# A decoder of two layers on one core: the second attention's masked keys made in three steps (batch 0, batch 1, batches 2 and 3) instead of two

## What is computed

```python
x = x + _L0_attn_ref(_layernorm(x), ...)                        # chunked delta rule with decays
x = x + _L0_xattn_ref(_layernorm(x), ctx_1024, ctx_1024, ...)   # 16 heads, tanh layers for q, k, v
x = x + _L0_ffn_ref(_layernorm(x), ...)                         # 4 experts, best 2
x = x + _L1_attn_ref(_layernorm(x), ...)                        # latent attention, causal
x = x + _L1_xattn_ref(_layernorm(x), ctx_1024, ctx_1024, ...)   # 16 heads, causal
x = x + _L1_ffn_ref(_layernorm(x), ...)                         # 8 experts, best 2
```

```python
latent = x @ Wc_down
q = (latent @ Wq_up).reshape(Bsz, Tlen, N_HEAD, HEAD_DIM)
kv = latent @ Wkv_up
k, v = (kv[..., :HEAD_DIM], kv[..., HEAD_DIM:])
att = jnp.einsum('bthd,bsd->bhts', q, k) * scale
att = jnp.where(causal[None, None], att, -jnp.inf)
att = jax.nn.softmax(att, axis=-1)
y = jnp.einsum('bhts,bsd->bthd', att, v).reshape(Bsz, Tlen, C)
return y @ Wc_proj
```

## Time and profile before

| | us |
|---|---|
| median of 3 runs | 5426.35 |
| lowest and highest of them | 5419.66, 5430.18 |
| the profiled execution, its own time | 5424.35 |
| its span, first to last instruction | 5421.6 |

### The profile page before, as it was taken

The page is one execution under the profiler, slowest core; times in us unless marked ns, Lnnn a source line. Parts: engine busy times, 40 slices in busy tenths (PEclk is TensorE's granted clock), DMA queues, the critical chain, the costliest instruction groups (busy, mean ns, idle before and its releaser), DMA issues.

```text
span 5421.6 us, 105836 instructions
## 1 busy us (share of the span) xinstructions
PE 4688.4 (86%) x28201; PEld 3073.6 (57%) x28362; DVE 4177.1 (77%) x10963; ACT 2323.3 (43%) x4480; POOL 4005.8 (74%) x11220
## 2 busy tenths in 40 slices
PE   1059998999999899999989999898999999899998
PEld 1045664656566565656656565565656556565655
DVE  7068787787887778788787878778787887778788
ACT  0034444444444444444444444444444444444344
POOL 7878676786867678686767868677786867768686
PEclk7589999999999999999999999999999999999999
DMA  3000000000000000000000000000000000000000
GB/s 97 0 13 1 29 1 13 17 9 21 1 25 5 9 21 9 21 1 25 5 9 21 7 23 1 25 5 9 21 1 29 1 25 5 9 21 1 21 1 17
DMA packets 61879, 78.07 MB, mean 14 GB/s; under 512 B 11168, under 2 KB 53808, under 8 KB 61232
## 3 DMA queue, kind: packets, MB, share of 16 engines
q1 hardware_dynamic: 52784, 62.42, 3.5%
q10 hardware_dynamic: 8448, 8.39, 0.4%
HBM read 45.04 MB, written 8.46 MB: 10 GB/s over the span
## 4 chain that ended last, share of the span: by engine, by line
POOL 36%; PE 28%; DVE 17%; issue 11%; ACT 4%; POOLq 3%; DMA 0%; DVEq 0%; ACTq 0%; SPq 0%
POOL acc_c L584 12%; POOL arena L584 7%; POOL acc_a L584 3%; POOL acc_b L584 3%; PE bank L1280 3%; POOL acc_s L584 3%; POOL sl_t L584 3%; POOLq L583 3%; PE bank L1016 2%; DVE arena L2018 2%; PE bank L1187 2%; PE bank L1023 2%; PE bank L1140 2%; PE bank L1106 2%; ACT arena L779 2%
## 5 line engine op out<-in xcount | busy, mean ns | idle before, releaser
L1784 DVE TENSOR_REDUCE smax<-bank 128x4 f32<-128x512 f32 x768 | 524.4, 683 | 92.1 <-PE bank L1098 31.8
L766 ACT ACTIVATE arena<-bank 128x512 f32<-128x512 f32 x768 | 454.8, 592 | 248.4 <-PE bank L1106 242.6
L1788 DVE TENSOR_TENSOR arena<-bank,smax 128x512 f32<-128x512 f32 x768 | 530.8, 691 | 26.4
L1106 PE MATMUL bank<-ident,arena 128*128 128x128 f32 x3072 | 484.8, 280 | 45.1 <-ACT arena L753 28.1
L1092 PE MATMUL bank<-arena 64*128 64x512 f32 x1536 | 439.2, 648 | 64.4 <-ACT arena L790 28.0
L1187 PE MATMUL bank<-w,arena 128*128 128x512 f32 x1024 | 480.0, 599 | 14.0 <-DVE arena L1736 14.0
L1106 PEld LDWEIGHTS bank<-ident,arena 128*128 128x128 f32 x3072 | 345.7, 141 | 245.0 <-ACT arena L755 82.3
L1220 PE MATMUL bank<-w,arena 128*128 128x256 f32 x2048 | 454.1, 380 | 13.9 <-ACT arena L825 13.9
L753 ACT ACTIVATE arena<-arena,rstd 128x512 f32<-128x512 f32 x512 | 368.2, 719 | 201.4 <-DVE arena L1788 196.8
L1220 PEld LDWEIGHTS bank<-w,arena 128*128 128x128 f32 x2048 | 387.8, 190 | 90.3 <-issue 23.0
L584 POOL TENSOR_TENSOR acc_a<-acc_s,arena 128x32 f32<-128x32 f32 x1008 | 264.6, 262 | 171.6 <-DVE row L1347 47.2
(11 more groups left out here) (428 smaller groups left out, 11813.6 us busy)
## 6 DMA issues: line engine op xcount, KB each, us to landing
arena<-in_x_dram SPq DMA_DIRECT2D x35, 512.0 KB, 3.6
xn_next<-arena SPq DMA_DIRECT2D x17, 512.0 KB, 2.9
arena<-cum_dram SPq DMA_DIRECT2D x17, 512.0 KB, 3.6
arena<-in_ctx_dram SPq DMA_DIRECT2D x16, 512.0 KB, 3.7
out_dram<-arena ACTq DMA_DIRECT2D x16, 512.0 KB, 3.1
xn<-xn_next SPq DMA_DIRECT2D x15, 512.0 KB, 3.1
w<-in_L_ffn_w_dram SPq DMA_DIRECT2D x8, 512.0 KB
w<-in_L_ffn_w_dram SPq DMA_DIRECT2D x1, 1024.0 KB
```

Of the source, the lines that this page charges most:

```text
L766: act.activation(PT[:, v % 2], bank[3 + v % 2][:, :].rearrange("p (h q) -> p h q", h=QH), ACT.Copy).then_inc(S["pt"], 1)
L1106: ins = tr(bank[3 + v % 2][:, j * P:(j + 1) * P], Ssb[:, v % 4, j, :], ident[:, :])
L1784: dve.tensor_reduce(smax[:, u, :], sc, AX, ALU.max).then_inc(S["s_max"], 1)
L1788: dve.tensor_tensor(Ssb[:, u % 4], sc, smax[:, u, :].unsqueeze(2).broadcast_to([P, QH, P]), ALU.subtract).then_inc(S["s_sub"], 1)
```

## The change

ACT makes the masked keys of the second attention for batch 0 alone, then for batch 1 alone, then for batches 2 and 3 together: twelve activations instead of eight, three raises of `km` instead of two. PE waits for the raise that belongs to its batch. The third attention's masks count from the fifth raise on.

```diff
@@ -54,7 +54,7 @@
-    h_psum=6, h_act=6, lat_psum=1, lat=1, q_psum=6, q=6, k_psum=5, k_rows=1, km=6, v_psum=5, v=6,
+    h_psum=6, h_act=6, lat_psum=1, lat=1, q_psum=6, q=6, k_psum=5, k_rows=1, km=7, v_psum=5, v=6,
@@ -784,10 +784,9 @@
                     act.wait_ge(S["k_psum"], at(it, "k_psum", 3))
-                    for m in range(2):
-                        two = slice(2 * m, 2 * m + 2)
+                    for some in (slice(0, 1), slice(1, 2), slice(2, 4)):
                         for j in range(QH):
-                            ins = act.activation(KM[:, two, 0, j, :], heads(bank[3][:, :])[:, two, :], ACT.Identity, scale=halfmask[:, j:j + 1])
+                            ins = act.activation(KM[:, some, 0, j, :], heads(bank[3][:, :])[:, some, :], ACT.Identity, scale=halfmask[:, j:j + 1])
                         ins.then_inc(S["km"], 1)
@@ -1084,7 +1083,7 @@
-                            pe.wait_ge(S["km"], at(it, "km", KM_BEFORE[a_no] + (c if chunks > 1 else g // 2) + 1))
+                            pe.wait_ge(S["km"], at(it, "km", KM_BEFORE[a_no] + (c if chunks > 1 else min(g, 2)) + 1))
@@ -2040,7 +2039,7 @@
-KM_BEFORE = (0, 2, 4)
+KM_BEFORE = (0, 2, 5)
```

## The result

The changed kernel took **5454.65 us** (median of 6 runs, 5451.20 to 5457.48) where the kernel before took 5428.31 (6 runs, 5419.66 to 5431.64): a ratio of **1.0048**, 95% interval 1.0037 to 1.0059. That is slower than the forecast 5429 and beyond the range's 5439. The same kernel measured once more in a later series gave 5444.44 us (10 runs, 5440.63 to 5448.50) beside 5433.46 (13 runs): 1.0021, interval 1.0012 to 1.0031. So the change costs between 0.2 and 0.5%, and how much differs from series to series by more than either interval.

The account below looks back on a forecast made before the run. POOL's chain to `au` was taken as the bound, absorbing the 0.40 us gain in DVE's wait. Sum: 5424.35 profiled - 0.4 (pass without wait) + 3.1 (one more long pass) + 2.0 (median above profile) = 5429 us; range 5417 to 5439.

Parts of the forecast that it names:

- The bound of the kernel: From the first mixture's gates to `au`, POOL's chain sets the pace, about 145 us; time gained before DVE's wait is absorbed.
- rival 1: The wait for `au` does not absorb the gain: 0.40 us shorter per pass, 6.4 us in all, 5420; chance 0.08.
- The masks: Second attention on ACT: narrow masks take 387 ns, all twelve end at 3.66 us, later batches do not wait.
- The shift: Second attention's first scores start 0.40 us earlier in each pass, with ends of 0 and 0.72.
- the register row ahead of the first scores: Added register operation on PE, covered by the wait for ACT; register rows taken as 0, bounds 0 and 2.6 us.
- The idle time before L1147: PE's idle time before the third batch's normalized attention grows by 0.40 us, 1.29 to 1.69, just under 1.77.
- the alternating case: Part of rival 2: passes of 1.69 us idle tip, the next does not; 8 long passes for 5, 5435.
- The count of long passes: Five of 15 passes were long, about 320 us; the change was taken to add one more.
- The clock term: PE's lost clock behind the wait before line 1148: 3.1 us per long pass, one more taken, +3.1 us.
- Rival 2: PE's longer idle time before line 1148 tips the clock in more passes: 5435 or 5445; chance 0.22.
- rival 3: The shift clears two or three long passes, one of which came with DVE late: 5417 to 5420; chance 0.12.
- What I said would show it: DVE's wait for `au` up 0.40 us a pass to about 24 in all; no growth means DVE not earlier.

Follow-up runs that it names:

- the wide mask first: Changed kernel with its three mask steps reordered: batches 0 and 1 together, then 2, then 3; 5429.85 us, ratio 0.9994 to the kernel before.
- POOL late: Kernel before, with two unread additions on POOL right before it writes `au`; 5454.43 us, ratio 1.0046.
- the repeat: The changed kernel measured once more in a later series, nothing edited; 5444.44 us, ratio 1.0021.
- the change's waits filled: Changed kernel with six unread matmuls in PE's wait before the third batch's transposes in the third attention; 5434.09 us, ratio 1.0000.
- both places: Changed kernel with twelve unread matmuls in PE's wait before line 1148 and 18 instead of 14 in the first mixture; 5406.03 us, ratio 0.9964.
- one then three: Kernel before with masks still in two steps, batch 0 alone, then batches 1, 2 and 3 together; 5456.87 us, ratio 1.0037.
- the mixture's fill alone: Changed kernel with 18 instead of 14 unread matmuls in the first mixture, none before line 1148; 5457.49 us, ratio 1.0048.
- the third fill: Changed kernel with both places filled, plus four unread matmuls before the last mixture's gates; 5406.52 us, ratio 0.9964.

## Why the prediction was wrong

- **The bound of the kernel**: right. POOL's stretch to `au` is 145.61 us on the mean after the change (145.52 before) and stays in 145.3 to 146.0. A gain in front of it was not worth anything: rival 1 (5420) came in no run of these masks without a new fill.
- **The masks**: right. 383 ns for the forecast 387, 3.63 us for twelve where 3.66 was figured (the wide ones read 537 ns instead of 488 behind narrow ones, but start 0.36 us apart as before), no wait for the later batches, and ACT's added time free (the wide mask first: 0.9994).
- **The shift**: too small. 0.52 us for 0.40, inside its ends of 0 and 0.72. The masks gave 0.42 where 0.40 was figured; the handover to PE gave another 0.09, and no term stood for it. I had put the register row ahead of the first scores at 0, and it goes with a gain.
- **The idle time before L1147**: wrong through the shift. I figured 1.69 and called it just under the 1.77 that had lost the clock. It was 1.78 to 2.17 in the long passes of both profiles but one (3.38). With the right shift the sum would have read 1.29 + 0.52 = 1.81, above 1.77, and the alternating case the least to expect. Even 1.69 would hardly have held: 1.51 lost the clock in both passes that had it (POOL late).
- **The count of long passes**: this is the step that failed. I took one more (+3.1 us); of all 16 there were nine more in the first profile (four by PE's idle time, five late) and six more in the second (five and one), the last pass among them. The clock term of the sum was 3.1 us, and the added long passes took 30.6 of the first profile's 31.6 us and about 18 of the repeat's 19.9. The price of one, 3.1 us, was right: 2.8 by the events behind `au`, 2.9 by the pair of the repeat.
- **What the count rested on**: I argued that a long pass shifts what follows it, from the one pair 1.96 and 0.97. In the repeat a long pass follows a long one with 1.97 to 1.98 four times (its second, eighth, ninth and twelfth).
- **Rival 2** was the mechanism, and I gave it 0.22. Its two prices, 5435 and 5445, frame the repeat: 5426.35 x 1.0021 = 5438. The first measurement, 5426.35 x 1.0048 = 5452, lies beyond both, and its profile has five late passes more, for which no term of the sum stood, though the profile before had one and rival 3 named it.
- **Rival 3**: it did not show. The register rows cost nothing (the wide mask first, 0.9994).
- **What I said would show it**: the wait for `au` was to grow to about 24 us. It went to 17.7 and 19.9, which by my own words would have said that DVE did not arrive earlier. It did: late passes with no wait at all took it out of the sum. The wait of single passes was the sign to name, 1.0 us in the short ones and 1.5 to 1.9 in those of kind (a), the fifth of the first profile with 3.1 apart, beside the late ones' count.

The Trainium skill's "TensorE: Matmul & The Clock Gate", section "HAM oscillation — how this bites in real kernels", says that waits between groups of matmuls start the next group cold. The traces agree for idle times of 1.51 to 3.48 us and not for those of 0.96 to 1.34. It was what decided here: late `au` alone, 1.0046, of which its own delay is 0.0023; the change's waits filled, 1.0000 and, with both places, 0.9964. The rule of the Trainium skill's "Perfetto Trace Analysis", section "Optimizing Scalar/DVE Operations", that broken-up instructions may let work finish sooner, holds up to the next wait only: the scores started 0.52 us sooner and the program ended later.

## What to carry to other kernels

Before starting a branch earlier, find the wait in which it ends, and ask what the engine with the granted clock does during that wait: the idle time grows by all that is gained, and 0.5 us more of it cost 3 us in each pass that lost the clock by it, four or five of 16 here. Where such a wait can't be removed, unread matmuls in it hold the clock, and they belong in every such wait at once, since a fill in one moved the idle time or the low clock to another place (apart 0 and 0.5%, together 0.8%). Where idle times stand near the one that loses the clock, count the passes at each level in more than one execution before giving a range.

## What the runs showed of the hardware

- In the six profiles without a new fill (before, after and its repeat, the wide mask first, one then three, POOL late) the idle time at L1147 parts the 81 passes in which DVE waited for `au` without an exception: with 0.96 to 1.34 us the clock held, 30 passes, and with 1.51 to 3.48 it fell, at the end of the idle time or right behind it, 51 passes. With the mixture's fill alone this line moves: 2.75 to 2.90 us kept the clock in five passes and 3.17 to 3.37 lost it, so the length alone doesn't decide.
- An idle time of 2 us mostly brings two low stretches, one right behind it and one some 34 us later, and they cost about as much each (1.35 and 1.45 us). Where the second is missing (after, second pass) the pass is of 319.7 us instead of 320.5.
- A low clock is free where another engine sets the end: 6.7 us at 0.50 behind the attention, and the pass of 317.4 to 317.5 us with it or without it.
- The scatter of the runs went with the clock: 5405.38 to 5407.60 us in six runs with both waits filled, where the profile has no long pass, and 5419.66 to 5431.64 in six of the kernel before, with five. With the third fill it came back: 5404.68 to 5430.79, and the profile of the slowest has low stretches 184 and 205 us behind the gates. Only one execution of each has a trace, so this is seen and not shown.
